# Two granules of the first half behind every second step, in place of one behind every step, in a depthwise-convolution and rotation kernel

## What is computed

```python
def _gn(v, G=32, eps=1e-05):
    g = v.reshape(B_, G, C_ // G, H_, W_)
    m = jnp.mean(g, axis=(2, 3, 4), keepdims=True)
    s = jnp.var(g, axis=(2, 3, 4), keepdims=True)
    return ((g - m) / jnp.sqrt(s + eps)).reshape(v.shape)

x = x + _L0_conv_ref(_gn(x), L0_conv_weight)       # depthwise 5x5 convolution
x = x + _L1_conv_ref(_gn(x), L1_conv_rota_matrix)  # einsum('hvc,bchw->bvhw', R, feats)
```

## Time and profile before

| | |
|---|---|
| time, median of 3 runs | 428.61 us (428.40 to 429.36) |
| the profiled execution | 428.04 us, span 426.2 us |
| busy, share of the span | PE 96%, DVE 85%, ACT 62%, POOL 57% |
| DMA | 139.83 MB, mean 328 GB/s |
| chain that ended last | PE 89%, POOL 3%, DMA 2%, issue 2% |

### The profile page before, as it was taken

The page is one execution under the profiler, slowest core; times in us unless marked ns, Lnnn a source line. Parts: engine busy times, 40 slices in busy tenths (PEclk is TensorE's granted clock), DMA queues, the critical chain, the costliest instruction groups (busy, mean ns, idle before and its releaser), DMA issues.

```text
span 426.2 us, 8616 instructions
## 1 busy us (share of the span) xinstructions
PE 407.3 (96%) x3110; PEld 200.7 (47%) x3110; DVE 362.2 (85%) x691; ACT 264.4 (62%) x513; POOL 242.6 (57%) x312
## 2 busy tenths in 40 slices
PE   7899999999999999999999999999999994999992
PEld 2345555555555555544444445444444541444440
DVE  4899999999999999889998889999887783687872
ACT  2386676667656775696666777666677534477760
POOL 7588675667656765696555676555553153344440
PEclk9999999999999999999999999999999998899997
DMA  8826579599977677977899999999999999999998
GB/s 295 374 58 226 213 221 316 220 334 380 373 250 281 241 272 270 341 255 245 339 360 372 301 384 344 352 391 330 411 361 394 407 377 386 401 427 427 424 425 344
DMA packets 36955, 139.83 MB, mean 328 GB/s; under 512 B 7472, under 2 KB 7600, under 8 KB 24368
## 3 DMA queue, kind: packets, MB, share of 16 engines
q1 hardware_dynamic: 17056, 107.29, 66.5%
q10 hardware_dynamic: 19856, 31.99, 20.8%
HBM read 72.14 MB, written 67.12 MB: 327 GB/s over the span
## 4 chain that ended last, share of the span: by engine, by line
PE 89%; POOL 3%; DMA 2%; issue 2%; DVE 1%; ACT 1%; ACTq 0%; SPq 0%; POOLq 0%
PE ps L743 61%; PE ps L778 26%; POOL area L447 2%; PE ps L784 2%; DMA kept<-x_scratch 1%; DMA norm<-affine 1%; DVE area L652 1%; PE ps L753 1%; PE ps L761 0%; ACT gn L542 0%; POOL gn L470 0%; POOL area L461 0%; ACTq L261 0%; DVE tin L652 0%; ACT std L514 0%
## 5 line engine op out<-in xcount | busy, mean ns | idle before, releaser
L743 PE MATMUL ps<-area 64*64 64x496 f32 (+2 forms) x2560 | 281.6, 586 | 2.4 <-POOL area L447 2.4
L743 PEld LDWEIGHTS ps<-area 64*64 64x64 f32 x2560 | 140.3, 133 | 98.4 <-issue 86.4
L447 POOL TENSOR_TENSOR area<-mask,area 128x325 f32<-128x325 f32 x128 | 132.3, 1056 | 44.3 <-PE ps L743 33.0
L778 PE MATMUL ps<-gn,rot 128*128 128x512 f32 x256 | 117.3, 611 | 6.2 <-ACT gn L542 5.9
L521 ACT ACTIVATE area<-area,affine 128x256 f32<-128x256 f32 x192 | 97.9, 588 | 34.4 <-DVE affine L632 32.5
L534 ACT ACTIVATE area<-ps 64x512 f32<-64x512 f32 x128 | 75.6, 591 | 31.2 <-PE ps L743 28.5
L610 DVE BATCH_NORM_STATS2 stats<-area 128x6 f32<-128x512 f32 x128 | 80.6, 689 | 3.8 <-DMA area<-in_x_dram 3.8
L778 PEld LDWEIGHTS ps<-gn,rot 128*128 128x128 f32 x256 | 48.3, 194 | 72.3 <-issue 60.4
L461 POOL TENSOR_SCALAR area<-area,affine 128x256 f32<-128x256 f32 x62 | 46.1, 752 | 63.3 <-DVE affine L632 63.2
L619 DVE BATCH_NORM_STATS2 stats<-area 128x6 f32<-128x512 f32 x128 | 81.1, 697 | 1.1
L652 DVE TENSOR_TENSOR tin<-ps,tin 128x512 f32<-128x512 f32 x68 | 46.8, 691 | 15.7 <-PE ps L778 15.6
(11 more groups left out here) (26 smaller groups left out, 110.3 us busy)
## 6 DMA issues: line engine op xcount, KB each, us to landing
area<-in_x_dram SPq DMA_DIRECT2D x31, 1024.0 KB, 6.5
x_scratch<-area ACTq DMA_DIRECT2D x29, 1024.0 KB, 7.4
out_dram<-tin SPq DMA_DIRECT2D x17, 1024.0 KB, 8.9
tin<-x_scratch SPq DMA_DIRECT2D x15, 1024.0 KB, 11.4
out_dram<-area SPq DMA_DIRECT2D x10, 1024.0 KB, 13.2
area<-x_scratch SPq DMA_DIRECT2D x7, 1024.0 KB, 11.8
rot<-in_rota_dram SPq DMA_DIRECT2D x4, 1024.0 KB, 9.1
kept<-x_scratch SPq DMA_DIRECT2D x16, 256.0 KB, 10.2
```

Source lines behind the costliest of these rows:

```text
L447: last = nc.gpsimd.tensor_tensor(taps[k % TRING][:, c * KW:(c + 1) * KW].rearrange("p d (b r) -> p d b r", r=TAPS), mask[:].rearrange("p d ...
L743: last = nc.tensor.matmul(ps[half, bank + c].rearrange("p (j w) -> p j w", j=J)[:, :, outs], taps[k % TRING][rows, (2 * pair + c) * KW + d ...
L778: nc.tensor.matmul(ps[:, rot_bank(m), :], rot[:, n % UNITS * RH + h], gn[n % NRING][:, h], start=True, stop=True).then_inc(rotated, 1)
```

## The change

Granules of the first half go in pairs behind steps 20, 22, 24, 26, 28, 29, 30 and 31 (`granules_of`), none behind 19, 21, 23, 25 and 27. Granule 15 stays behind the last convolution, where 13, 14 and 15 were. SyncE's list stores both granules of a pair together two turns later; its loads keep one granule a turn and take a second in turns 29, 30 and 31, and the waits for the buffer that they overwrite follow. Thirteen of the second half's granules are loaded in quarters instead of ten; the list at the end has their quarters, and its stores and loads of whole granules in another order. `tin` places granules 11 and following anew. ScalarE and GpSimd normalise the first granule of a pair one step ahead up to step 28 and in the same step from 29 on, there behind the normalising of the next step.

```diff
-KEPT = STEPS_ALL - START
+TWICE = STEPS_ALL - 3
-IN_QUARTERS = 10
+IN_QUARTERS = 13
...
-        tin = [own[n % DRING] for n in range(KEPT)] + [granule_on(at_x[n]) for n in (2, 3, 4)]
+        tin = [own[n % DRING] for n in range(11)]
+        tin += [granule_on(at_x[2]), own[3], granule_on(at_x[3]), own[0], granule_on(at_x[4])]
...
+        def granules_of(s):
+            if s < TWICE and s % 2 == 1:
+                return range(0)
+            first = s - START - 1 if s < TWICE else TWICE - START + 2 * (s - TWICE)
+            return range(first, first + 2)
-        LAST_THREE = KEPT * RH - 1
+        LAST_THREE = granules_of(STEPS_ALL - 1)[0] * RH
...
                 if START + 2 <= s < STEPS_ALL:
-                    store_granule(sp, s - START - 2)
+                    for n in granules_of(s - 2):
+                        store_granule(sp, n)
...
                 if s == STEPS_ALL:
                     store(sp, s - 2)
-                    store_granule(sp, 11)
+                    for n in granules_of(s - 2):
+                        store_granule(sp, n)
                     load_norms(1)
-                n = s - START + 1
-                if 2 <= n < KEPT:
+                if START + 1 <= s < STEPS_ALL - 1:
+                    n = s + 1 - START if s + 1 <= TWICE else granules_of(s + 1)[0]
                     if n >= DRING:
-                        sp.wait_ge(out_stored[n - DRING], 16)
+                        sp.wait_ge(out_stored[{12: 7, 14: 8}.get(n, n - DRING)], 16)
                     load_granule(sp, n)
-                n = s - 29 + KEPT
-                if KEPT <= n < UNITS:
+                if s >= TWICE and s < STEPS_ALL:
                     await_stores(sp, s - 3)
                     sp.wait_ge(stats_ready, measured(s - 3 + LAG))
-                    load_granule(sp, n)
+                    load_granule(sp, granules_of(s)[1])
...
                 if s == STEPS_ALL - 1:
-                    for n, left in ((20, 9), (22, 10)):
+                    for n, left in ((20, 9), (21, 10), (22, 11)):
                         sp.wait_ge(out_stored[left], 16)
                         for r in range(QUARTERS - 1):
                             load_quarter(sp, n, r)
             await_stores(sp, STEPS_ALL - 3)
             sp.wait_ge(stats_ready, measured(STEPS_ALL - 3 + LAG))
             for r in range(QUARTERS - 1):
-                load_quarter(sp, 21, r)
+                load_quarter(sp, 25, r)
+            for n, left in ((23, 12), (24, 13)):
+                sp.wait_ge(out_stored[left], 16)
+                for r in range(QUARTERS - 1):
+                    load_quarter(sp, n, r)
             sp.wait_ge(convolved, 2 * STEPS_ALL)
             for r in range(QUARTERS - 1):
-                load_quarter(sp, 23, r)
+                load_quarter(sp, 26, r)
             store(sp, STEPS_ALL - 1)
-            for n in (24, 25):
+            for n in (27, 28):
                 for r in range(QUARTERS - 1):
                     load_quarter(sp, n, r)
-            store_granule(sp, 12)
             await_stores(sp, STEPS_ALL - 1)
             for n in range(UNITS, UNITS + IN_QUARTERS):
                 load_quarter(sp, n, QUARTERS - 1)
-            load_granule(sp, 26)
-            store_granule(sp, 13)
...
         @block.gpsimd
...
-                if s + 1 >= START:
-                    normalise_rows(s + 1 - START)
-            for n in range(KEPT, GRANULES):
+                if s >= TWICE:
+                    normalise_rows(granules_of(s)[0])
+                if s >= START and granules_of(s):
+                    normalise_rows(granules_of(s)[1])
+                if START < s + 1 < TWICE and granules_of(s + 1):
+                    normalise_rows(granules_of(s + 1)[0])
+            for n in range(granules_of(STEPS_ALL - 1)[0], GRANULES):
                 normalise_rows(n)
         @block.scalar
...
+                if s >= TWICE:
+                    normalise_rows(granules_of(s)[0])
                 evict(s, 0)
                 store(act, s - 1)
-                if s + 1 >= START:
-                    normalise_rows(s + 1 - START)
+                if s >= START and granules_of(s):
+                    normalise_rows(granules_of(s)[1])
+                if START < s + 1 < TWICE and granules_of(s + 1):
+                    normalise_rows(granules_of(s + 1)[0])
             s = STEPS_ALL - 1
             evict(s - 1, 1)
             take_root(s + 1)
-            normalise_rows(KEPT)
+            normalise_rows(UNITS - 2)
             send_norms(act, s - 3)
             evict(s, 0)
+            normalise_rows(UNITS - 1)
             evict(s, 1)
...
         @block.vector
...
-                add_rows(s - START, range(RH))
+                for n in granules_of(s):
+                    add_rows(n, range(RH))
...
         @block.tensor
...
                 if s >= START:
-                    rotate(s - START, range(RH))
+                    for n in granules_of(s):
+                        if n < UNITS - 1:
+                            rotate(n, range(RH))
             last_round = ROUNDS - 1
-            rotate(KEPT, (0, 1))
+            rotate(UNITS - 1, (0, 1))
...
```

More of the change, by code:

```diff
@@ L115, in granule_on @@
             return piece(a, (RH, J * W))
-        tin = [own[n % DRING] for n in range(KEPT)] + [granule_on(at_x[n]) for n in (2, 3, 4)]
+        tin = [own[n % DRING] for n in range(11)]
+        tin += [granule_on(at_x[2]), own[3], granule_on(at_x[3]), own[0], granule_on(at_x[4])]
         tin += [kept[:, n] for n in range(FRONT)]
-        tin += [own[1], granule_on(at_x[5]), own[2], granule_on(at_n[0]), granule_on(at_n[1]), granule_on(at_t),
-                granule_on(at_t + TILE), granule_on(at_x[0]), own[3], granule_on(at_x[1]), own[0], granule_on(at_x[2])]
+        tin += [own[1], own[2], granule_on(at_x[2]), own[3], granule_on(at_x[3]), granule_on(at_x[5]),
+                granule_on(at_n[0]), granule_on(at_n[1]), granule_on(at_t), granule_on(at_t + TILE),
+                granule_on(at_x[0]), granule_on(at_x[1])]
         near, near_middle = gn[0][:, 0, 0:HALF + BAND], gn[0][:, 1, 0:HALF + BAND]
@@ L379, in _ @@
                 load_quarter(sp, n, QUARTERS - 1)
-            load_granule(sp, 26)
-            store_granule(sp, 13)
[L382 to L385, removed]
             store_granule(sp, 14)
             load_granule(sp, 29)
-            sp.wait_ge(out_stored[12], 16)
+            store_granule(sp, 15)
+            sp.wait_ge(stats_ready, measured(ROUNDS - 1))
             load_granule(sp, 30)
-            store_granule(sp, 15)
-            sp.wait_ge(out_stored[13], 16)
             load_granule(sp, 31)
@@ L577, in _ @@
             send_norms(act, s - 2)
-            normalise_rows(KEPT + 1)
             take_root(s + 3)
-            normalise_rows(KEPT + 2)
             send_norms(act, s - 1)
             send_norms(act, s)
-            for n in range(KEPT + 3, GRANULES):
+            for n in range(UNITS, GRANULES):
                 normalise_rows(n)
@@ L710, in _ @@
             measure_sum(s)
-            add_rows(KEPT - 1, (0, 1))
+            add_rows(UNITS - 2, (0, 1))
             deviate(s + 3)
-            add_rows(KEPT - 1, (2,))
+            add_rows(UNITS - 2, (2, 3))
             scale(s + 3)
-            add_rows(KEPT - 1, (3,))
-            for n in range(KEPT, GRANULES):
+            for n in range(UNITS - 1, GRANULES):
                 add_rows(n, range(RH))
@@ L819, in _ @@
                 if s >= START:
-                    rotate(s - START, range(RH))
+                    for n in granules_of(s):
+                        if n < UNITS - 1:
+                            rotate(n, range(RH))
             last_round = ROUNDS - 1
-            rotate(KEPT, (0, 1))
+            rotate(UNITS - 1, (0, 1))
             for half in (low, high):
                 average_mean(last_round, half)
-            rotate(KEPT, (2, 3))
+            rotate(UNITS - 1, (2, 3))
             for half in (low, high):
                 average_spread(last_round, half)
-            for n in range(KEPT + 1, GRANULES):
+            for n in range(UNITS, GRANULES):
                 rotate(n, range(RH))
```

## The result

The kernel after takes 434.1 us (median of 4 runs, 433.75 to 435.67), the kernel before on the same chip 428.99. The ratio is 1.0125 with a 95% interval of 1.0095 to 1.0156: slower by about 5.4 us. The forecast was 439.5 us, with a range of 433.2 to 446.0; the profiled execution moved by 6.2 us of span, from 426.2 to 432.4, where the sum said 10.9.

The account below looks back on a forecast made before the run. The prediction took the path last convolution, sum written, stored, its quarter loaded, normalised, through SyncE's fixed-order queue, as the bound. Its terms, 7.26 + 1.1 + 4.8 - 2.3 = +10.9 us, gave 439.5 us, range 433.2 to 446.0.

Parts of the forecast that it names:

- the low end: Lower bounds of the terms taken together, 7.26 + 0 + 1 - 3.7 = +4.6 us, so 433.2 us.
- Two more granules in front and the late normalising: Steps 29 to 31: two more granules before the last convolution's end, +7.26 us; late normalising in step 29, +1.1 us.
- the alternating steps: Steps 20 to 28, pairs in place of single granules: no TensorE stall, cost zero, upper end 1.5 us.
- SyncE between the last two sums: SyncE's queue before store(31): one more granule's store and six more quarter loads, 0.55 + 4.26 = +4.8 us, bounds 1 and 9.
- paced by the queue, not by themselves: Argument that SyncE's extra issues could hide: today's quarter issues vary between 0.63 and 1.01 us.
- From the last quarter to granule 16: From the first last-quarter load's issue to TensorE's start on granule 16: left at 9.13 us, no change.
- The tail: Sixteen granules on TensorE behind the gap: 58.18 us as before, same clock loss.
- The end: Last half store lands sooner on a nearly empty queue, 4.6 us in place of 6.9: -2.3 us, bounds 0 and -3.7.
- the third rival: Tail paced by DMA, so fewer bytes left to move there make the kernel faster: 425 us, chance 0.05.
- SyncE's waits in the steps: Loads of granules 4, 6, 8 and 10 wait for just-issued stores, about 6.4 to 8.9 us: cost zero.
- The first rival: SyncE's extra issues hide because less is queued, and the last store lands at its best: 434.5 us, chance 0.20.

Follow-up runs that it names:

- e12: The kernel after with each pair's stores at the end of the turn before, as in e11, and e5's end: 429.43 us, ratio 1.0021.
- e6: The kernel after with store(31) first and eighteen quarters, of granules 23 to 28, moved behind the last quarters: 435.49 us, ratio 1.0147.
- e2: The kernel before with only pairs behind steps 20 to 28, single granules behind 29 to 31, SyncE's end as before: 427.62 us, ratio 0.9986.
- e1: The kernel after with store(31) moved ahead of the quarters of 25, 23, 24 and 26 in SyncE's list: 433.32 us, ratio 1.0121.
- e5: The kernel after with store(31) first and the nine quarters of granules 26, 27 and 28 behind the last quarters: 431.09 us, ratio 1.0061.
- e11: The kernel after with the two stores of a pair at the end of SyncE's turn before: 431.81 us, ratio 1.0067.
- e9: The kernel after with some granule and quarter loads moved one SyncE turn sooner, to turns 29 and 30: 438.09 us, ratio 1.0236.

## Why the prediction was right, point by point

The direction and the place, TensorE's gap in front of granule 16, were right, and the time lies in the range, near its low end. The mechanism was right in part: the last sum comes later, and what follows it stands longer at SyncE, but not for the reason given. The sum of the terms was 4.7 us too high, and that the time is in the range is partly luck: the low end stood on a cost of 1 us at SyncE and none in step 29, which came out at 5.4 and 0.85, and 3.2 us that the sum had left as they were (step 28's earlier end, the last quarter's sooner landing) made up for most of that. Term by term, on the profiled executions:

- **Two more granules in front and the late normalising: +8.4 forecast, +6.95 measured** (last sum at 347.74 in place of 340.79). The wait in step 29 is 0.85 us (1.1 forecast). Step 28 ends 1.15 us sooner than I assumed: without a granule in step 19 a wait of 0.48 us for GpSimd there is gone, and two granules in a row take 7.08 us, not 7.26. That the whole of this term lies on the path, as the prediction said, e12 does not bear out: with the same late sum granule 16 starts only 3.6 us later than before and the span ends 1.1 us later. In the kernel before, 19.2 us lie between the last sum and granule 16, in e6 14.6 us, so part of a later sum can be taken in there. In the alternating steps TensorE's waits for VectorE's addition come to 0.3 us in all; e2 shows that this costs no time.
- **SyncE between the last two sums: +4.8 forecast, and this is the step that was reasoned wrongly.** "For store(31) waits the whole tail" was the reason, and store(31) is indeed 6.3 us later behind its sum. e1 shows that this lateness is worth nothing: the store can leave at once and granule 16 does not move. What the tail waits for is the last quarter, which stands behind the other quarters as well as behind store(31): with nine of them fewer in front, e5 starts granule 16 6.3 us sooner than after, and 6.4 us sooner than e1. Both readings of the term, 0.71 us an issue and 4.05 us of bytes, count these quarters, so that its size came out near, and no run separates them. That issues are "paced by the queue, not by themselves" holds for the slow ones alone, as e6 shows. From the last sum to the last quarter's issue it is 15.46 us in place of 10.04, so +5.4.
- **From the last quarter to granule 16: no change forecast, 2.05 us less measured** (7.08 in place of 9.13; the quarter lands in 4.30 us in place of 6.36). This I had left as it was. I had kept 7.93 us for store(31) too; it took 7.05, and that is in the 15.46.
- **The tail: no change forecast, 58.0 against 58.18 us.** Right: in every profile TensorE sets it, without a gap and by its granted clock.
- **The end: -2.3 forecast, -3.9 measured** (8.06 us behind the last matmul to 4.12). I took a 256 KB load as the nearest row for a 512 KB store. The Trainium skill, page "DMA: Bandwidth & Descriptors", Anatomy of one DMA, gave an estimate of 3.2 us; the profile after shows 3.2. (The page's fit is for DMAs that GpSimd issues, and SyncE issues this store; here it agrees.)

Together 6.95 + 5.4 - 2.05 - 0.2 - 3.9 = +6.2 us, the difference of the spans.

What the prediction did not see is the second wall. It priced the third rival, a tail on DMA, only as a gain for the change, and put SyncE's waits in the steps at zero because the granules would still be in time for TensorE. They are in time, but the bytes that are not moved then come due later: in front of the last quarters, or behind the last addition. e11 and e12 show that about 4.5 of the 5.4 us lost hang on SyncE's list (by the ratios e5's order 2.7, the stores sooner 2.5 alone, 4.5 together; each of these differences is good to some 1.5 us). The first rival, "the queue takes it in", comes nearest to the time (434.5), but not for its reason: the queue did not hide the bytes; the end, step 28 and the quarter's landing gave more back.

What stays open: the last 0.9 us of e12 were not taken apart; no run tells the bytes of the quarters in front from SyncE's time to issue them, or kept ten granules in quarters; and no run moved only TensorE's two granules with SyncE's list of before, since the buffers of granules 13 to 15 and the loads go together.

## What to carry to other kernels

Where transfers fill the DMA engines from some point to the end, count what stands in front of the one that is waited for, and the bytes moved by a given time, before counting places in an issuing queue: in e1 a store moved to the front gained nothing, for what was awaited came behind the same quarters. A finished store that waits for the next turn of a loop leaves a hole that is paid later, so issue it when it is ready, and put nothing in front of it that waits for something younger. A kernel can stand at two walls at once; after an edit, the drain behind the last computation (3.4 us or much more) told here which one it ended on.

## What the runs showed of the hardware

A DMA issue on SyncE is not a fixed cost: 256 KB quarters that follow each other mostly took about 0.6 us each, also with DMA at a share of 0.26 and 60 GB/s (four in 2.57 us in e6), and the first four in e1, at a share of 1.00, took 1.02 to 1.35 us. An estimate from the four in e6: a quarter every 0.65 us is some 400 GB/s, so SyncE handing out quarters of this size is about as fast as DMA in the tail (387 to 419 GB/s), and which of the two held the start is hard to tell. Time to landing is not fixed either: a 1 MiB store of a sum took 4.9 us in e12 (issued at 347.98) and 15.9 in e9 (issued at 292.31), and the 512 KB stores at the end 3.2 us after the change and 6.9 before. A DMA share of 1.00 is not one rate: it stood beside 388 GB/s in the gap after the change, 392 from 304 to 340 us before it and 419 in the tail before it, so the share alone does not tell whether bytes can still be won. And the idle of TensorE in front of the tail, 16.8 us in place of 6, cost no more clock: the granted clock over the tail is 0.95 in both, after 0.56 on average in the gap. Over all profiles it lies between 0.95 and 1.00, and that alone makes the tail 55.2 to 58.2 us long.
